# Five of 32 input products of the Mamba scans made by TensorE from six chunks on, weight and column loads in pieces, and two silus in separate slots

## The chip, the cores and the metric

The kernel runs on one core of a Trainium2 chip. The time is that of the whole launch in microseconds of the device, as the median of three runs. The engines are PE (TensorE), DVE (VectorE), ACT (ScalarE), POOL (GpSimd) and SP (SyncE, which here only issues transfers). Each takes its own instructions strictly in the order in which they are written.

## What is computed

Four layers of a network over x of 2 batches, 1024 tokens, 256 features. Layer 0 is a Mamba block, layer 1 a bidirectional one (a forward and a backward scan), layers 2 and 3 are attention. The scans of layers 0 and 1 are what the change touches:

```python
xt = jnp.transpose(x_in, (0, 2, 1))                       # layer 0 only: convolution over 4 tokens, then silu
u = jax.nn.silu(conv(xt) + conv_b)
x_dbl = jnp.einsum('bsd,ed->bse', u, x_proj_w)
dt_r, B, C = jnp.split(x_dbl, [DT_RANK, DT_RANK + N], axis=-1)      # N = 16 states
dt = jax.nn.softplus(jnp.einsum('bsr,dr->bsd', dt_r, dt_proj_w) + dt_proj_b)
def step(h, inp):
    dA = jnp.exp(dt_t[:, :, None] * A)
    h = h * dA + (dt_t * u_t)[:, :, None] * B_t[:, None, :]
    y = jnp.einsum('bdn,bn->bd', h, C_t)
    return (h, y)
y = (y + u * D_param) * jax.nn.silu(z)                    # z: the second half of the input projection
```

There are 512 channels and 16 states, so each token has 512 x 16 values of h.

## The kernel before, in words

**Chunks and steps.** The scans are cut into 12 chunks of 512 tokens (`WORK`, `NK` = 12): chunks 0 to 3 are layer 0 (two batches of two chunks), chunks 4 to 7 layer 1 of the first batch (forward 4 and 5, backward 6 and 7), chunks 8 to 11 the same of the second. A chunk has 32 steps (`HALVES`): two halves of the channels (256 channels each, as two blocks q = 0 and 1 of 128 partitions) times 16 states n. `at` counts all 384 steps, `h` those of a chunk. A chunk is "second" where it carries h on from the one before (1, 3, 5, ...). In the others ("first") ACT keeps the last value of each scan (`save`, L1976), and POOL waits for that.

**One step** goes through the engines like this:

1. PE `spread` (L1577): one matmul of 48 rows copies row n of B to all 128 partitions, into PSUM bank 2 or 3 in turn. It waits until DVE has read that bank two steps ago.
2. DVE `load` (L2161): w (= dt times u, in `ws`) times that bank, 128x1024, into a slot of `hbuf`, a ring of five (`RING`).
3. ACT `decays` (L1968): exp(dt * A) for q = 0 and q = 1, each 128x512, into PSUM bank 6 + q. It waits for the scan of the step before, which read that bank.
4. DVE `scan` (L2176): two scans of 128x512, q = 0 and q = 1, in place in the ring, with the bank of decays as factor.
5. POOL weighs the slot with row n of C (L1340), 128x1024, from `cbuf`, a ring of three that SP fills by `load_c` (L1094), 256 KB each. `load_c` of a step waits until POOL has weighed three steps ago.
6. PE `add_state` (L1598): four matmuls of 64x64 add the slot to the sums in banks 0 and 1.

**The order is written by hand.** In pass h of its loop, DVE runs load(at + 1) and scan(at), ACT the decays of at, POOL its product of at, PE spread(at + 2) and add_state(at - 2), SP load_c(at). After that each engine does the work "beside" the scan that falls due at slot h: generators `beside(j)` yield slot numbers, and what stands behind a yield is issued at that slot. These hold the projections of the next chunk (z at slots 4, 6, 8, 10 of a chunk ahead of a backward one, L1429; the projection to B, C and dt at 21 or 22, L1456; dt, L1463), the output projection of the last one (L1405), the layer norms of chunks 4, 5, 8 and 9 (in the chunk before each: POOL's L1219 and L1221 at slots 7 and 8, DVE's statistics of their result at slot 10, L2064), POOL's four products for dt and w at slot 27 (L1252, L1258), POOL's tap of the convolution in layer 0 (L1203, L1207, L1209), and the silus. For these ACT has to load another table and then the old one again (`silus`): z (L1729), then u (L1737) in layer 0. The decays of one step (`AHEAD`, slot 21 or 14) are made before that, into two spare banks.

**Loads beside chunk 0.** At slot 12 SP stores the conditioning, loads all weights of layer 1 (`in_w` to `wl1`, L1112, 3968 KB in one), two rows (L1076) and four small columns (`f_ada`, L1082, each of 512 single elements of 4 bytes). Its next `load_c` stands behind these. The columns of layers 2 and 3 are first read in chunk 2, the weights in chunk 3.

In the code block below, the lines are those of the profile.

## Time and profile before

| | us |
|---|---|
| median of three runs | 2138.95 (2136.35 to 2139.67) |
| the profiled execution | 2137.9 |
| its span, first to last instruction | 2136.1 |
| the scans, first load to last scan | 68.7 to 1477 |
| attention, after the scans | about 1479 to 2136 |
| mean granted clock of TensorE | 0.848 of full |

The chunks begin (first scan) at 72.4, 202.1, 320.6, 440.8, 565.6, 680.5, 791.9, 900.5, 1022.1, 1136.2, 1247.8 and 1357.0 us. A step takes 3.36 us in a first and 3.48 us in a second chunk where nothing is beside it. The profile gives the busy time of each engine, the waits with who ended them, and the instructions in order of time.

### The profile page before, as it was taken

Reading aid. Unit: us, or ns where it says so; the run is one execution under the profiler, and the core shown is the slowest. Engines: PE = TensorE matmul, PEld = TensorE weight load, DVE = VectorE, ACT = ScalarE, POOL = GpSimd, SP = SyncE. Lnnn points to the kernel's source line nnn. Section 1 sums busy time; section 2 is a strip of 40 time slices with the busy share of each in tenths; the row PEclk is TensorE's granted clock in tenths of the full one; section 3 lists DMA queues with packets and bytes.
Section 4 is the critical chain, followed back from the end, with each engine's and each line's share of the span. In section 5 each row is a group of like instructions: output and inputs, shape, how many; then the busy total and the mean of one; then the engine's idle time right before and its main releaser. Section 6 shows DMA issues by size and latency. Waiting matters only on the chain.

```text
span 2136.1 us, 22565 instructions
## 1 busy us (share of the span) xinstructions
PE 1728.3 (81%) x7664; PEld 588.8 (28%) x7664; DVE 1854.2 (87%) x2189; ACT 1199.4 (56%) x2147; POOL 1147.4 (54%) x584
## 2 busy tenths in 40 slices
PE   5776979789797777778787878787887899999986
PEld 2221313133231211122221112232663333333323
DVE  4688999899999999999999999999557888888803
ACT  3756565645656565555565655553462266666672
POOL 2667977877888887778888786864000000000000
PEclk9887979859687788878778778797998799999998
DMA  5142222122222222212222222321060522220001
...
DMA packets 80727, 143.41 MB, mean 67 GB/s; under 512 B 14587, under 2 KB 19643, under 8 KB 80076
## 3 DMA queue, kind: packets, MB, share of 16 engines
...
## 4 chain that ended last, share of the span: by engine, by line
DVE 46%; PE 33%; issue 10%; ACT 5%; POOL 4%; DMA 1%; SPq 1%; DVEq 0%; ACTq 0%; POOLq 0%
DVE hbuf L2176 27%; DVE hbuf L2161 11%; PE psum L688 6%; PE psum L654 5%; PE psum L674 4%; PE psum L1598 4%; PE psum L569 3%; POOL hbuf L1340 3%; DVE gain L969 2%; PE psum L558 2%; PE psum L1429 1%; PE psum L1405 1%; PE psum L1554 1%; PE psum L1577 1%; PE psum L1456 1%
## 5 line engine op out<-in xcount | busy, mean ns | idle before, releaser
L1340 POOL TENSOR_TENSOR hbuf<-hbuf,cbuf 128x1024 f32<-128x1024 f32 x384 | 902.1, 2356 | 286.6 <-DVE hbuf L2176 147.0
L1968 ACT ACTIVATE psum<-slots,cols 128x512 f32<-128x512 f32 x768 | 525.3, 687 | 450.6 <-DVE hbuf L2176 446.8
L1598 PE MATMUL psum<-hbuf,ident 64*64 64x512 f32 x3072 | 530.1, 768 | 211.6 <-POOL hbuf L1340 211.2
L2161 DVE TENSOR_TENSOR hbuf<-slots,psum 128x1024 f32<-128x1024 f32 x384 | 459.4, 1197 | 52.8 <-POOL slots L1258 30.3
L2176 DVE TENSOR_TENSOR_SCAN hbuf<-psum,hlast,hbuf 128x512 f32<-128x512 f32 x384 | 470.4, 1266 | 3.1 <-ACT psum L1968 3.0
L2176 DVE TENSOR_TENSOR_SCAN hbuf<-psum,hbuf 128x512 f32<-128x512 f32 x384 | 447.4, 1206 | 4.5 <-ACT psum L1968 4.4
L969 DVE TENSOR_REDUCE gain<-psum 128x1 f32<-128x512 f32 x512 | 315.7, 682 | 59.1 <-PE psum L654 58.7
L520 POOL COPY wl<-hbuf 128x512 f32<-128x512 f32 x8 | 4.8, 612 | 429.3 <-PE psum L688 400.7
L654 PE MATMUL psum<-slots 99*128 99x512 bf16 x512 | 197.1, 400 | 23.9 <-DVE gain L969 11.5
L1577 PE MATMUL psum<-bcs,pick 48*128 48x512 bf16 x384 | 171.0, 446 | 45.0 <-DVE hbuf L2161 42.8
L674 PE MATMUL psum<-slots 102*128 102x512 bf16 x512 | 194.4, 388 | 6.5 <-ACT xn_flat L852 1.7
L1598 PEld LDWEIGHTS psum<-hbuf,ident 64*64 64x64 f32 x3072 | 94.7, 154 | 366.7 <-POOL hbuf L1340 305.2
L852 ACT ACTIVATE slots<-psum 128x512 f32<-128x512 f32 x256 | 133.9, 626 | 62.4 <-PE psum L674 62.4
L1577 PEld LDWEIGHTS psum<-bcs,pick 48*128 48x128 bf16 x384 | 36.8, 96 | 378.8 <-DVE hbuf L2161 228.1
L852 ACT ACTIVATE xn_flat<-psum 128x512 f32<-128x512 f32 x128 | 70.3, 607 | 81.2 <-PE psum L674 81.2
L1429 PE MATMUL psum<-slots,wl 128*128 128x512 f32 x192 | 107.3, 693 | 0.0
L674 PEld LDWEIGHTS psum<-slots 102*128 102x128 bf16 x512 | 49.4, 98 | 141.6 <-issue 50.3
L654 PEld LDWEIGHTS psum<-slots 99*128 99x128 bf16 x512 | 51.3, 100 | 85.9 <-DVE gain L969 45.9
L1976 ACT ACTIVATE hlast<-hbuf 128x2 f32<-128x2 f32 x192 | 39.5, 206 | 63.0 <-DVE hbuf L2176 62.4
L688 PE MATMUL psum<-slots,wl 128*32 128x512 f32 x512 | 67.9, 651 | 7.4 <-issue 7.4
L1405 PE MATMUL psum<-w_gated,slots 128*128 128x256 f32 x256 | 68.4, 416 | 6.1 <-DVE slots L2184 6.1
L852 ACT ACTIVATE wl<-psum 128x512 f32<-128x512 f32 x128 | 71.0, 625 | 3.6 <-PE psum L674 3.5
...
## 6 DMA issues: line engine op xcount, KB each, us to landing
cbuf<-scr_c SPq DMA_DIRECT2D x384, 256.0 KB, 3.1
...
```

The source lines that it names most:

```text
L654: pe.matmul(psum[:, 4 + n % 4, :], st[0:K_MAX, 0, h, i * P:(i + 1) * P], st[0:K_MAX, 1, h, side * 512:side * 512 + 512], start=True, stop= ...
L674: pe.matmul(psum[:, 1 + n % 3, :], st[0:K_EXP, 1, h, i * P:(i + 1) * P], st[0:K_EXP, 0, h, a * 512:a * 512 + 512], start=True, stop=True). ...
L688: last = pe.matmul(psum[h * 32:h * 32 + 32, 0, :], v_quad[job % 2][:, ip * 2 + il, h, :], probs[g % 2][h][:, il * 512:il * 512 + 512], sta ...
L852: act.activation(probs[g % 2][h][:, il * 512:il * 512 + 512], psum[:, 1 + n % 3, :], ACT.Exp).then_inc(exped, 1)
L969: dve.tensor_reduce(half_max[:, n % 2, at:at + 1], psum[:, 4 + n % 4, :], AX.X, ALU.max).then_inc(maxed, 1)
L1340: pool.tensor_tensor(hs, hs, cbuf[:, at % CRING:at % CRING + 1, :].to_broadcast([P, 2, TC]), ALU.mult).then_inc(weighed, 1)
L1429: last = pe.matmul(ps, w[:, m, at:at + P], src[:, m, :], start=m == 0, stop=m == KD - 1)
L1577: pe.matmul(psum[:, 2 + at % 2, :], pick[:, n:n + 1].to_broadcast([3 * NS, P]), bcs[0:3 * NS, k % 2 * TC:(k % 2 + 1) * TC], start=True, st ...
L1598: last = pe.matmul(psum[side, bank, :], ident[rows_of, rows_of], hbuf[rows_of, at % RING, q, :], start=False, stop=n == NS - 1, skip_group ...
L1968: act.activation(decay_bank(at, q), dts[k % 2][:, e, :], ACT.Exp, scale=coefficient(WORK[k], e, n)).then_inc(decay, 1)
L2161: dve.tensor_tensor(hbuf[:, at % RING, :, :], ws[k % 2][:, 2 * p:2 * p + 2, :], psum[:, 2 + at % 2:3 + at % 2, :].to_broadcast([P, 2, TC]) ...
L2176: dve.tensor_tensor_scan(hs, decay_bank(at, q)[:, way], hs, hlast[:, e, n:n + 1] if c.second else 0.0, ALU.mult, ALU.add).then_inc(scanned, 1)
```

## The change

**Products by PE.** In chunks 5 to 10 (`PE_CHUNKS`) the steps h = 9, 11, 13, 27 and 29 (states 9, 11 and 13; `PE_SLOTS`) have no load and no spread. PE makes the product of w and B instead (`product`): for each q and each block of 128 tokens one matmul, f32, 128x128x128, with the transposed w (`wT`) as weights and a matrix that has B of the state on its diagonal (`diag_b`) as the moving side. q = 0 goes into bank 2 or 3, where the spread would have gone, q = 1 into bank 7. The scan reads this from PSUM and its decays from the ring slot in SBUF, where ACT now writes them. product(at, 0) is written in pass at - 1 behind add_state, product(at, 1) at the head of pass at, and it waits for the scan of step at - 1 to have read bank 7. The spread of the step after a run of such steps is written one pass later than before.

**What feeds it.** For each chunk PE turns four blocks of w (`turn_w`, four 128x128 transposes each, at slots 2, 3 and twice at 14 or 16), and ACT copies them out (`turned_w`, four of 128x512). SP writes three rows of B as the diagonals of three DRAM matrices (`store_diagonals`, 512 elements of 4 bytes each, slots 27, 29, 31 of the chunk before) and loads the three matrices, 256 KB each, at slot 3. The DRAM area is filled with zeros once (1.5 MB, slot 8 of chunk 1) from a small tile that POOL clears first. POOL's and ACT's split of B writes its remainder elsewhere, so that B stays; shapes and counts are as before.

**Loads.** The weights of layer 1 are loaded in eight pieces at slots 13 to 20 of chunk 0, and the four column loads stand in chunk 1, at slots 8, 9, 14 and 19 (the first yields 4, but stands behind the clearing at 8).

**Silus.** For chunks 1 to 3, ACT does the silu of u at slot 20 and that of z at slot 21; the table loads are the same two.

```diff
+PE_CHUNKS = range(5, NK - 1)
+PE_STATES = (9, 11, 13)
+PE_SLOTS = (9, 11, 13, 27, 29)
+def by_matmul(at):
+    k, h = divmod(at, HALVES)
+    return k in PE_CHUNKS and h in PE_SLOTS
...
         def decay_bank(at, q):
+            if by_matmul(at):
+                return hbuf[:, at % RING, q, :]
...
+        def product_bank(at, q):
+            return psum[:, 7 if q else 2 + at % 2, :]
...
+            def store_diagonals(k):
+                for i, n in enumerate(PE_STATES):
+                    yield 27 + 2 * i
...
+                    sp.dma_start(on_diagonal, values, allow_slow_non_contiguous=True).then_inc(diag_stored, 16)
...
+                if j in PE_CHUNKS:
+                    yield 3
+                    load_diagonals(j)
...
                 if j == 0:
                     yield 12
                     store_conditioning(1)
                     sp.wait_ge(grouped, done("ada", 1, 0))
-                    sp.dma_start(wl1[:, 0:NW1], w1).then_inc(ld_w1, 16)
                     load_conditioning_rows()
-                    load_film_columns()
+                    for n in range(W1_PIECES):
+                        yield 13 + n
+                        piece = slice(n * NW1 // W1_PIECES, (n + 1) * NW1 // W1_PIECES)
+                        sp.dma_start(wl1[:, piece], w1[:, piece]).then_inc(ld_w1, 16)
+                if j == 1:
+                    yield from load_film_columns()
...
+            def product(at, q):
+                k, h = divmod(at, HALVES)
+                p, n = divmod(h, NS)
+                i = PE_STATES.index(n)
+                pe.wait_ge(taken_act, taken(G["wT", k, 2 * p + q]))
+                pe.wait_ge(ld_diag[i], 16 * (k - PE_CHUNKS[0] + 1))
+                if q:
+                    pe.wait_ge(scanned, 2 * (at - 1) + 2)
+                else:
+                    before = max(m for m in range(at % 2, at, 2) if not by_matmul(m))
+                    pe.wait_ge(dbu, loaded(before))
+                    if by_matmul(at - 2):
+                        pe.wait_ge(scanned, 2 * (at - 2) + 1)
+                for j in range(TB):
+                    last = pe.matmul(product_bank(at, q)[:, j * P:(j + 1) * P], wT[:, j, q * P:(q + 1) * P], diag_b[i][:, j * P:(j + 1) * P],
+                                     start=True, stop=True)
+                last.then_inc(dbu_matmul, 1)
...
                     at = j * HALVES + h
-                    if at + 2 < TOTAL:
+                    if by_matmul(at - 1) and not by_matmul(at + 1):
+                        spread(at + 1)
+                    if by_matmul(at):
+                        product(at, 1)
+                    elif at + 2 < TOTAL and not by_matmul(at + 2):
                         spread(at + 2)
                     if at >= 2:
                         add_state(at - 2)
+                    if by_matmul(at + 1):
+                        product(at + 1, 0)
...
                         ahead(k)
-                        silus(k)
+                        act.preload_act_table_set("silu_and_others")
+                        silu_of_u(k)
+                        yield SILU0 + 1
+                        silu_of_z(k)
+                        act.preload_act_table_set("natural_log_exp_and_others")
...
-                    if at + 1 < TOTAL:
+                    if at + 1 < TOTAL and not by_matmul(at + 1):
                         load(at + 1)
```

PE in chunk 6, slots 7 to 10, before: L1577 is the spread, L1598 add_state (64x512 x4), L1429 the projection of z.

```order
L1577 MATMUL psum<-bcs,pick 128x512
L1598 MATMUL psum<-hbuf,ident 64x512 x4
L1577 MATMUL psum<-bcs,pick 128x512
L1598 MATMUL psum<-hbuf,ident 64x512 x4
L1429 MATMUL psum<-slots,wl 128x512 x2
L1577 MATMUL psum<-bcs,pick 128x512
L1598 MATMUL psum<-hbuf,ident 64x512 x4
```

The same place in the change: L1673 is the spread, L1721 add_state, L1510 z, L1699 the product.

```order
L1721 MATMUL psum<-hbuf,ident 64x512 x4
L1673 MATMUL psum<-bcs,pick 128x512
L1721 MATMUL psum<-hbuf,ident 64x512 x4
L1699 MATMUL psum<-wl 128x128 x4
L1510 MATMUL psum<-slots,wl 128x512 x2
L1699 MATMUL psum<-wl 128x128 x4
L1721 MATMUL psum<-hbuf,ident 64x512 x4
L1673 MATMUL psum<-bcs,pick 128x512
```

The spreads of steps 9 and 11 are gone; product(9, 0) has come between add_state and the projection of z, product(9, 1) behind it.

ACT in chunk 0, slots 20 to 22, before: L1968 x2 are the decays ahead, L1729 the silu of z, L1737 that of u, L1976 the save.

```order
L1968 ACTIVATE psum<-slots,cols 128x512 x2
L1742 ACT_TABLE_LOAD
L1729 ACTIVATE slots<-slots 128x2048
L1737 ACTIVATE slots<-slots 128x2048
L1747 ACT_TABLE_LOAD
L1976 ACTIVATE hlast<-hbuf 128x2
L1968 ACTIVATE psum<-slots,cols 128x512
```

In the change: L2119 are decays, L1873 the silu of u, L1865 that of z, L2127 the save.

```order
L2119 ACTIVATE psum<-slots,cols 128x512 x2
L1943 ACT_TABLE_LOAD
L1873 ACTIVATE slots<-slots 128x2048
L2127 ACTIVATE hlast<-hbuf 128x2
L1865 ACTIVATE slots<-slots 128x2048
L1947 ACT_TABLE_LOAD
L2119 ACTIVATE psum<-slots,cols 128x512
```

One save has come between the two silus, and u is first.

SP in chunk 0 at slot 12, before, and then the change (there L1113 is the store, L1119 the rows, L1138 load_c, L1189 a piece of the weights):

```order
L1070 DMA scr_ada<-slots 2x1792
L1112 DMA wl<-in_w 128x7936
L1076 DMA wl<-scr_ada 128x768 x2
L1082 DMA f_ada<-scr_ada 128x4x1 x4
L1094 DMA cbuf<-scr_c 128x512 x14
```

```order
L1113 DMA scr_ada<-slots 2x1792
L1119 DMA wl<-scr_ada 128x768 x2
L1138 DMA cbuf<-scr_c 128x512
L1189 DMA wl<-in_w 128x992
L1138 DMA cbuf<-scr_c 128x512
```

The weights now come in pieces between the load_c, and the column loads have left this chunk.

## Rows read from the trace of the kernel before

**Rows 1.** The page: busy us, share of the span and instructions of each engine

```profile
PE 1728.3 (81%) x7664; PEld 588.8 (28%) x7664; DVE 1854.2 (87%) x2189; ACT 1199.4 (56%) x2147; POOL 1147.4 (54%) x584
```

**Rows 2.** Waits of DVE: waited for, us in total, times, longest

```profile
DVE hbuf L2161 <- POOL slots L1258: 30.3, 1, 30.3
DVE hbuf L2161 <- PE psum L1577: 22.4, 9, 8.3
DVE hbuf L2176 <- ACT psum L1968: 7.4, 12, 2.4
```

**Rows 3.** Timeline, end of chunk 7: start, us, engine, line, [idle before <-releaser]

```profile
1007.07 1.20 DVE L2161 TENSOR_TENSOR hbuf<-slots,psum 128x1024 f32<-128x1024 f32 x1
...
1008.18 2.45 DVE L2176 TENSOR_TENSOR_SCAN hbuf<-psum,hlast,hbuf 128x512 f32<-128x512 f32 x2
...
1009.50 0.69 ACT L1968 ACTIVATE psum<-slots,cols 128x512 f32<-128x512 f32 x1 [1.06 <-DVE hbuf L2176]
...
1010.55 1.20 DVE L2161 TENSOR_TENSOR hbuf<-slots,psum 128x1024 f32<-128x1024 f32 x1
```

**Rows 4.** Busy time in chunks 5 to 10, all engines, then L2161 alone

```profile
680.00:1357.00 677.00, 523.39 (x2188) 134.10 (x2184) 675.80 (x625) 400.37 (x694) 550.11 (x265) 0.78 0.25 76
...
680.00:1357.00 677.00, 230.23 (x193) 0.78 0.25 76
```

**Rows 5.** Timeline, SP's queue at the start and in chunk 0, POOL, DVE

```profile
22.74 0.94 SPq L1145 DMA_DIRECT2D ada_cols<-scr_ada  x2
...
116.88 10.53 SPq L1082 DMA_DIRECT2D f_ada<-scr_ada  x4
...
132.83 2.34 POOL L1340 TENSOR_TENSOR hbuf<-hbuf,cbuf 128x1024 f32<-128x1024 f32 x1 [8.68 <-DMA cbuf<-scr_c]
...
141.29 1.22 DVE L2161 TENSOR_TENSOR hbuf<-slots,psum 128x1024 f32<-128x1024 f32 x1 [8.32 <-PE psum L1577]
```

**Rows 6.** Timeline, chunk 0 around the silus: ACT, POOL, PE, DVE

```profile
159.75 1.89 ACT L1737 ACTIVATE slots<-slots 128x2048 f32<-128x2048 f32 x1
...
163.31 6.96 POOL L1340 TENSOR_TENSOR hbuf<-hbuf,cbuf 128x1024 f32<-128x1024 f32 x3 [6.95 <-ACT hlast L1976]
...
167.61 5.65 PE L1456 MATMUL psum<-slots 128*96 128x512 f32 x8
...
163.84 2.34 DVE L2176 TENSOR_TENSOR_SCAN hbuf<-psum,hbuf 128x512 f32<-128x512 f32 x2 [2.39 <-ACT psum L1968]
...
173.62 1.22 DVE L2161 TENSOR_TENSOR hbuf<-slots,psum 128x1024 f32<-128x1024 f32 x1 [4.08 <-PE psum L1577]
```

**Rows 7.** Timeline, chunk 2 around the silus: POOL and DVE

```profile
398.87 1.26 POOL L1209 TENSOR_TENSOR slots<-slots 128x512 f32<-128x512 f32 x1
...
405.06 1.22 DVE L2161 TENSOR_TENSOR hbuf<-slots,psum 128x1024 f32<-128x1024 f32 x1 [5.19 <-PE psum L1577]
```

**Rows 8.** Timeline of PE: transposes, then chunk 6 around slot 8

```profile
961.75 1.94 PE L1419 MATMUL psum<-ident,xn_flat 128*128 128x128 f32 x8
...
1503.89 1.91 PE L551 MATMUL psum<-ident,wl 128*128 128x128 f32 x16
...
817.51 1.98 PE L1598 MATMUL psum<-hbuf,ident 64*64 64x512 f32 x8 [1.59 <-POOL hbuf L1340]
819.43 3.78 PE L1429 MATMUL psum<-slots,wl 128*128 128x512 f32 x4
823.14 0.59 PE L1577 MATMUL psum<-bcs,pick 48*128 48x512 bf16 x1
823.65 1.09 PE L1598 MATMUL psum<-hbuf,ident 64*64 64x512 f32 x8
```

**Rows 9.** Timeline of POOL and DVE at slots 8 to 10, chunks 7 and 8

```profile
942.52 2.35 POOL L1221 TENSOR_TENSOR xn_flat<-xn_flat,shift 128x1024 f32<-128x1024 f32 x1
...
944.98 1.38 DVE L2064 BATCH_NORM_STATS2 stats<-xn_flat 128x6 f32<-128x256 f32 x4
...
1062.67 1.41 DVE L2064 BATCH_NORM_STATS2 stats<-xn_flat 128x6 f32<-128x256 f32 x4 [0.53 <-POOL xn_flat L1221]
```

122 lines of the change are left out of this document (104 added, 18 removed).

## The prediction, as it was put on record

> **What bounds the kernel now.** I read the busy shares first [rows 1]: DVE leads with 87%, PE follows with 81%. A share over the whole span hides the stages, so next come the windows over chunks 5 to 10 [rows 4]: of 677 us DVE is busy 675.8, PE 523, POOL 550, ACT 400. There DVE is the bound and nobody makes it wait. The waits of DVE [rows 2] say the same from the other side: in the whole scan stage loads waited for PE only 9 times, 22.4 us in total, 8.3 of it in one place, and scans for ACT 7.4 us. So a gain can come from DVE instructions taken away in chunks 5 to 10, and from those few waits in chunks 0 to 3. The attention behind the scans is not touched; it moves as a whole.
>
> **The price of a load.** In a quiet step [rows 3] a load starts at 1007.07, the pair of scans at 1008.18, the next load at 1010.55. The instructions overlap a little, so a load costs 1.11 us of DVE's time, not its 1.20, and a pair of scans 2.37. The change removes 5 loads in each of 6 chunks: 30 x 1.11 = 33.3 us. The scan still reads one operand from PSUM and one from SBUF (they change places), so I leave its price; whether the place of the operands matters no row shows, and I allow 0.1 us for each of 60 scans either way, 6 us, in the range. If all 30 loads came off the path and nothing else moved, that is the ceiling of this part.
>
> **Who must now be on time.** Without a load in front, scan(at, 0) follows scan(at - 1, 1) at once, and two engines lose slack.
>
> ACT: it starts its decays 0.06 us after the scan that frees the bank and takes 0.69 (the pair of scans starts at 1008.18, its first is over at about 1009.44, ACT starts at 1009.50) [rows 3]. With as much for the way back it needs about 0.85 us, the scan in between lasts 1.18. That fits, by 0.3 us (0.2 with a save ahead of it). I take nothing for it. The copies of the turned w (four of about 0.7 a chunk) and the split of B with its new address stand beside scans in ACT's and POOL's idle time; nothing.
>
> PE: four products or transposes of 128x128 f32 take 0.96 us at the full clock (16 records, two for each matmul, in 1.91) and 1.94 at half of it (8 in 1.94) [rows 8]; add_state 1.09 and 1.98, a spread 0.59 at half clock (0.4 I take at full). A step of this kind adds 8 matmuls and drops one spread, and a chunk adds 16 transposes: 5 x 1.9 + 3.9 - 5 x 0.4 = 11.4 us at full clock, to 87 of 113 us (523/6) [rows 4]. So PE has the room on average, and the question is order. Product(at, 1) may start when scan(at - 1, 1) is over and is wanted after one load and one scan, 1.11 + 1.18 = 2.3 us later; alone it fits at either clock. Where a z projection stands between product(at, 0) and it (slots 8 and 10 of chunks 5, 6, 9, 10), it does not always. In chunk 6 [rows 8] add_state starts at 817.51 and z runs 3.78 us from 819.43, at the half clock up to about 823.6. With product(9, 0) ahead of z, z ends at about 824.4 and product(9, 1) at 825.4; DVE, with load(9) gone, wants it at about 822.2. That is 3.2 us lost against 5.55 won in this chunk. The same walk gives 1.3 in chunk 5, 1.5 in chunk 10 and 0.5 in chunk 9, where PE keeps the full clock. Sum 6.5. At slots 27 and 29 PE now gets work where it ran at half clock before; at full clock everything fits, in the first microseconds at half clock up to 1 us may go. I take 2 us for six chunks.
>
> **A gain that cannot be had.** In chunks 7 and 8 DVE's statistics at slot 10 wait for POOL's L1221. In chunk 7 it ends at 944.87 and DVE starts at 944.98 with no idle time, just in time; in chunk 8 DVE already waits 0.53 us [rows 9]. POOL is busy without a gap ahead of this, so it doesn't come earlier. Two loads (9 and 11) go ahead of that place, so 2 x 1.11 in each of two chunks is turned into waiting: 4.4 us.
>
> Chunks 5 to 10: 33.3 - 6.5 - 2.0 - 4.4 = 20.4 us.
>
> **Loads of chunk 0.** The four column loads hold SP's queue for 10.53 us [rows 5], while two column loads of the same form, with no weights ahead of them, took 0.94. So it is the queue full of 3968 KB of weights that holds them, and load_c stands behind. POOL waits 8.68 for its row of C, and DVE, by way of PE, 8.32 for POOL: one chain. With pieces of 496 KB between the load_c, each an eighth of that, 1.3 us, and the columns elsewhere, all of the 8.32 goes. What is late next is POOL with its convolution, as in chunk 1, where DVE's only waits of over 0.3 us are one for ACT; all its waits for PE are nine [rows 2]. In chunk 1 the clearing of 1.5 MB and four column loads of 0.5 us come in. The clearing takes some 4 to 6 us of the queues, my estimate from the 10.53 us for which 3968 KB held them; POOL is behind its convolution there and asks for rows late. Nothing, at worst 2 us.
>
> **Silus.** In chunk 0 POOL waits 6.95 us for the save behind both silus; add_state, and behind it the projection L1456 (5.65 us at half clock), come late, and DVE waits 4.08 for its spread [rows 6]. With the save between the silus it comes where the second silu started, at 159.75, and POOL starts at about 160.1 and not 163.31: 3.2 us earlier, and so does PE. I take 3.5 us with the clock that the shorter gap saves, between 2.5 and 4.4. The 2.39 us for the decays stay: ACT has the same work up to them. In chunk 2 the wait of 5.19 us isn't the silus': POOL does its whole convolution in one go there up to 400.1, and PE waits for POOL [rows 7]; that remains, and u now waits for the convolution with z behind it, by my walk without a loss. Chunk 1 is a second chunk without saves: nothing.
>
> **Sum.** 20.4 + 8.3 + 3.5 = 32.2 us off the profiled execution of 2137.9 gives 2105.7. The median of the runs lies 1.05 above that execution, so I predict **2106 us** (own range 2099 to 2114).
>
> **Rivals.**
>
> *All of it is had (2096).* If PE stays at the full clock in these chunks, the 6.5 and 2.0 shrink to about 0: 2106 - 8.5 = 2097, and with the last microsecond of the silus 2096. For it: the products fill PE's gaps. Against: at slot 8 of chunk 6 PE waited for POOL 1.59 us and ran at half clock though its share there was high [rows 8], and POOL's pace does not change. The Trainium skill, "TensorE: Matmul & The Clock Gate", Part 1, says that the throttled clock is the default and that activity releases it; by that rule more work makes each matmul cheaper, and the sum would be this one. In the rows PE goes back to the full clock at 823.6 after it has worked without a gap from 817.5, which agrees.
>
> *PE's order eats the products (2126).* One late product delays the scan, and add_state behind it keeps PE late for the next. If each of the 30 products costs as much as it saves, the 20.4 go: 2106 + 20 = 2126. For it: 3.2 us in a single place of chunk 6, and half clock at slots 26 to 31, where a product, two add_states and a spread (3.88 + 3.96 + 0.59) would take PE 8.4 us against the 5.85 of two DVE passes (2.37 + 3.48). Against: busy without a gap, PE should leave the half clock.
>
> *Slower (2155).* The transfers for the diagonals hold SP's queue, with load_c behind them. Place: three stores of 512 single elements at slots 27 to 31 and 768 KB of loads at slot 3, in each of six chunks. Price: in chunk 0 a hold of 10.53 us cost DVE 8.32 [rows 5], so 2.2 us are covered; six holds as long as that one cost 6 x 8.3 = 50, and 2106 + 50 = 2156, less the change of the places where POOL is behind anyway: 2155. It turns the change into a loss from 2.2 + 33/6 = 7.7 us of hold a chunk. Against: the columns of the same form took 0.47 us each to issue. These read from DRAM, though, and ours write to it; no row shows that. The Trainium skill, "DMA: Bandwidth & Descriptors", Specifications, says that below 512 B a transfer becomes a read-modify-write, which speaks for this rival; no row here shows such a store.
>
> *The edit in chunk 0 doesn't do what it says (2117).* If the wait there comes back elsewhere (the clearing in chunk 1, the pieces ahead of load_c), 8.3 + 3.5 go: 2118 with the products as forecast, 2117 with what the clock gives.
>
> **Chances.** Forecast 0.43, all of it 0.19, PE's order 0.20, chunk 0 0.07, slower 0.08; 0.03 for something that I don't see. The range is to hold 8 in 10: from 2094, which takes in the upper case and part of the 6 us of the scans, to 2128, which takes in PE's order; the slower case and the tails stay out. A measurement of this kernel tells apart about 0.2%, 4.3 us. Faster than that: all but the slower case, the unknown and a little of PE's order, 0.87; the same 0.04; slower 0.09.
>
> **What would show it.** In the profile of the change: 354 loads instead of 384, and chunks 5 to 10 together 656 to 657 us long instead of 676.5. Right: no DVE wait near 8 us in chunk 0, a wait of about 2.2 us of L2064 for POOL in chunk 7 and 2.7 in chunk 8, waits of scans for the products of 1 to 3 us at slot 9 of chunks 5, 6 and 10, none at 27 and 29. Wrong: POOL waiting for cbuf in chunks 5 to 11 (the slower rival), scans waiting for products at all five slots (PE's order), scans longer than 1.27 us, or scans waiting for ACT in each step without a load.

## The result and the profile after

| | before | after |
|---|---|---|
| median of the runs, us | 2138.99 (6 runs, 2136.35 to 2142.39) | 2122.32 (6 runs, 2116.56 to 2127.02) |
| profiled execution, us (span) | 2137.9 (2136.1) | 2122.75 (2121.0) |
| first scan starts, us | 72.4 | 73.2 |
| chunk 0, us | 129.7 | 115.3 |
| chunk 1, us | 118.5 | 124.2 |
| chunks 2 to 4, us | 359.9 | 359.7 |
| chunks 5 to 10, us | 676.5 | 668.8 |

The ratio is 0.992, with a 95% interval of 0.9907 to 0.9933: faster, by 16.7 us where I had forecast 33 (2138.95 to 2106). Chunk lengths run from the first scan of a chunk to the first scan of the next. Chunk 0 gave 14.4 us (forecast 11.8), chunks 5 to 10 gave 7.8 (forecast 20.4), and chunk 1 lost 5.7 (forecast nothing).

Where the products are, the window over chunks 5 to 10 answers to [rows 4]. Columns: the stretch, its length, then busy time and number of records of PE, PE's weight loads, DVE, ACT and POOL, the granted clock, DMA share and GB/s. Second, the waits of DVE in it (us in total, times, longest):

```profile
672.38:1341.17 668.79, 542.16 (x2734) 198.13 (x2730) 644.52 (x596) 410.24 (x717) 549.26 (x265) 0.90 0.29 84
```

```profile
DVE hbuf L2331 <- ACT psum L2119: 7.7, 8, 3.4
DVE hbuf L2331 <- PE psum L1699: 6.4, 6, 2.5
DVE stats L2215 <- POOL xn_flat L1301: 4.9, 2, 2.8
DVE hbuf L2312 <- PE psum L1673: 3.1, 4, 1.2
DVE hbuf L2312 <- issue: 1.7, 2, 1.0
```

(L2312 is the load, L2331 the scan, L1699 the product, L1673 the spread, L1721 add_state, L2119 a decay, L2132 the copy of the forward sums, L1421 POOL's weighing, L1301 its L1221 of before.) DVE's busy time fell from 675.8 to 644.5: the loads are gone. But DVE, which had waited 1 us in all, now waits 23.8. The gain was made and then three quarters of it turned into waiting, nearly half of that for decays and spreads (7.7 and 3.1 us), for which I had allowed 2 us at most.

In chunk 1 the clearing of the diagonals' buffer shows. First the DMA issues of 210 to 240 us (KB each, median us from issue to landing), then the chain on POOL, PE and DVE (start, us, engine, line, what, idle before and for whom):

```profile
scr_diag<-wl SPq DMA_DIRECT2D x1, 1539.0 KB, 19.3
cbuf<-scr_c SPq DMA_DIRECT2D x6, 256.0 KB, 6.6
f_ada<-scr_ada SPq DMA_DIRECT2D x2, 2.0 KB, 15.8
```

```profile
233.97 2.35 POOL L1421 TENSOR_TENSOR hbuf<-hbuf,cbuf 128x1024 f32<-128x1024 f32 x1 [7.20 <-DMA cbuf<-scr_c]
...
236.36 1.98 PE L1721 MATMUL psum<-hbuf,ident 64*64 64x512 f32 x8 [7.77 <-POOL hbuf L1421]
...
242.41 1.22 DVE L2312 TENSOR_TENSOR hbuf<-slots,psum 128x1024 f32<-128x1024 f32 x1 [5.28 <-PE psum L1673]
```

The clearing is 19.3 us on its way, and a load of 256 KB beside it takes 6.6 us to land, where in a quiet stretch (500 to 540 us, eleven loads) it takes 3.2. The hold on the queue that I feared for the small stores came from this one.

The other loss is at the start of chunk 9. PE, ACT and DVE there (its first scan is at 1120.84):

```profile
1111.38 0.60 PE L1673 MATMUL psum<-bcs,pick 48*128 48x512 bf16 x2
1117.13 1.99 PE L1721 MATMUL psum<-hbuf,ident 64*64 64x512 f32 x8 [5.16 <-POOL hbuf L1421]
...
1123.96 2.07 PE L1544 MATMUL psum<-wl,wdts 64*128 64x512 f32 x2
1125.82 0.63 PE L1673 MATMUL psum<-bcs,pick 48*128 48x512 bf16 x1
1126.38 1.98 PE L1721 MATMUL psum<-hbuf,ident 64*64 64x512 f32 x8
...
1128.43 1.02 ACT L2132 ACTIVATE slots<-psum 128x1024 f32<-128x1024 f32 x1 [4.42 <-PE psum L1721]
...
1131.30 1.28 DVE L2331 TENSOR_TENSOR_SCAN hbuf<-psum,hlast,hbuf 128x512 f32<-128x512 f32 x1 [3.43 <-ACT psum L2119]
```

Read it backwards. DVE waits for the decays of slot 2. They stand in ACT's queue behind the copy of the last chunk's sums, and that waits 4.42 us for PE's last add_state. PE is late because POOL had let it stand idle for 5.16 us and because, from 1117.13 on, it works at half clock (1.99 us for an add_state that takes 1.09 at the full one). The windows of the same stretch show the clock (length, PE busy, clock, DMA):

```profile
1113.20:1117.10 3.90, 0.00 (x0) 0.83 0.06 22
...
1117.13:1136.50 19.37, 19.37 (x65) 0.51 0.43 122
```

POOL, at last, is late because of what stands at its slot 27: two pairs of operations (1109.84 to 1114.74) and then five weighings in a row. At the end of the weighing of slot 28 its lag behind the scans was 6.2 to 6.9 us before and is 7.4 to 8.6 now. A part of this is DMA: in chunks 6, 7, 8 and 10 POOL waits 0.9 to 1.5 us for its row of C just ahead of these operations (before only once, 0.95 us in chunk 10). In chunks 5 and 9, where it doesn't wait, the lag still grew by 1.2 us. It catches up by a step's length less 2.35 us; a step without a load is 2.3 to 2.4 us long. So a load saved behind slot 27 takes POOL's time to catch up away.

### The profile page after: what moved, and what is told of

Its sections match the earlier page's. It is cut to its first block, busy times and chain, and to the rows that moved or that the text cites. A ratio compares the mean times of both kernels' runs of the same rounds, so it can differ in the third digit from the quotient of the medians.

```text
span 2121.0 us, 23810 instructions
## 1 busy us (share of the span) xinstructions
PE 1739.7 (82%) x8210; PEld 651.4 (31%) x8210; DVE 1822.9 (86%) x2159; ACT 1211.9 (57%) x2171; POOL 1147.5 (54%) x585
## 4 chain that ended last, share of the span: by engine, by line
PE 40%; DVE 34%; issue 9%; POOL 8%; ACT 7%; DMA 2%; SPq 0%; DVEq 0%; ACTq 0%; POOLq 0%
DVE hbuf L2331 19%; DVE hbuf L2312 7%; PE psum L1721 6%; PE psum L731 6%; POOL hbuf L1421 6%; PE psum L697 5%; PE psum L717 4%; PE psum L612 3%; PE psum L1510 3%; DVE gain L1012 2%; PE psum L601 2%; PE psum L1673 1%; PE psum L1518 1%; PE psum L1537 1%; DMA cbuf<-scr_c 1%
## 5 line engine op out<-in xcount | busy, mean ns | idle before, releaser
L1421 POOL TENSOR_TENSOR hbuf<-hbuf,cbuf 128x1024 f32<-128x1024 f32 x384 | 901.8, 2358 | 272.9 <-DVE hbuf L2331 141.2
L2119 ACT ACTIVATE psum<-slots,cols 128x512 f32<-128x512 f32 x708 | 485.5, 689 | 392.0 <-DVE hbuf L2331 387.9
L1721 PE MATMUL psum<-hbuf,ident 64*64 64x512 f32 x3072 | 491.6, 715 | 172.8 <-POOL hbuf L1421 172.2
L2312 DVE TENSOR_TENSOR hbuf<-slots,psum 128x1024 f32<-128x1024 f32 x354 | 422.1, 1193 | 49.8 <-POOL slots L1338 30.3
L2331 DVE TENSOR_TENSOR_SCAN hbuf<-psum,hlast,hbuf 128x512 f32<-128x512 f32 x354 | 432.5, 1263 | 8.7 <-ACT psum L2119 8.7
L2331 DVE TENSOR_TENSOR_SCAN hbuf<-psum,hbuf 128x512 f32<-128x512 f32 x354 | 411.1, 1200 | 8.8 <-ACT psum L2119 8.8
L697 PE MATMUL psum<-slots 99*128 99x512 bf16 x512 | 197.1, 400 | 23.9 <-DVE gain L1012 11.5
L1721 PEld LDWEIGHTS psum<-hbuf,ident 64*64 64x64 f32 x3072 | 91.0, 147 | 318.3 <-POOL hbuf L1421 255.4
L1673 PE MATMUL psum<-bcs,pick 48*128 48x512 bf16 x354 | 147.5, 423 | 34.2 <-DVE hbuf L2312 32.4
L1673 PEld LDWEIGHTS psum<-bcs,pick 48*128 48x128 bf16 x354 | 32.9, 95 | 291.3 <-issue 150.5
L1510 PE MATMUL psum<-slots,wl 128*128 128x512 f32 x192 | 104.8, 680 | 6.9 <-ACT wl L1833 6.9
L1699 PE MATMUL psum<-wl 128*128 128x128 f32 x480 | 70.8, 294 | 14.0 <-DVE hbuf L2331 10.4
L2127 ACT ACTIVATE hlast<-hbuf 128x2 f32<-128x2 f32 x192 | 39.7, 207 | 68.7 <-DVE hbuf L2331 68.4
L1699 PEld LDWEIGHTS psum<-wl 128*128 128x128 f32 x480 | 61.9, 201 | 46.9 <-issue 40.7
```

Source lines behind the costliest of these rows:

```text
L697: pe.matmul(psum[:, 4 + n % 4, :], st[0:K_MAX, 0, h, i * P:(i + 1) * P], st[0:K_MAX, 1, h, side * 512:side * 512 + 512], start=True, stop= ...
L1421: pool.tensor_tensor(hs, hs, cbuf[:, at % CRING:at % CRING + 1, :].to_broadcast([P, 2, TC]), ALU.mult).then_inc(weighed, 1)
L1510: last = pe.matmul(ps, w[:, m, at:at + P], src[:, m, :], start=m == 0, stop=m == KD - 1)
L1673: pe.matmul(psum[:, 2 + at % 2, :], pick[:, n:n + 1].to_broadcast([3 * NS, P]), bcs[0:3 * NS, k % 2 * TC:(k % 2 + 1) * TC], start=True, st ...
L1699: last = pe.matmul(product_bank(at, q)[:, j * P:(j + 1) * P], wT[:, j, q * P:(q + 1) * P], diag_b[i][:, j * P:(j + 1) * P], start=True, st ...
L1721: last = pe.matmul(psum[side, bank, :], ident[rows_of, rows_of], hbuf[rows_of, at % RING, q, :], start=False, stop=n == NS - 1, skip_group ...
```

## Experiments

All times are medians, with the ratio to the kernel before and its 95% interval. "5 to 10" is the length of these chunks in the profiled execution, 676.5 before. I lean on it more than on the medians, since the first scan starts at 72 us in some traces and at 77 in others (last section). But it is the length in one execution.

| kernel | us | ratio | 5 to 10 | loads gone there |
|---|---|---|---|---|
| the change | 2122.3 | 0.992 (0.9907 to 0.9933) | 668.8 | 30 |
| e1, clearing in pieces | 2119.1 | 0.9906 (0.989 to 0.9922) | 668.6 | 30 |
| e2, no products | 2126.1 | 0.9946 (0.9932 to 0.9959) | 676.5 | 0 |
| e3, slots 9, 11, 13 | 2128.2 | 0.9948 (0.9933 to 0.9963) | 672.2 | 18 |
| e4, slots 27, 29 | 2131.1 | 0.9958 (0.9943 to 0.9973) | 679.6 | 12 |
| e5, e1 + sums later | 2118.6 | 0.9908 (0.9895 to 0.9922) | 664.6 | 30 |
| e6, e1 + PE kept busy | 2119.6 | 0.9913 (0.99 to 0.9927) | 669.2 | 30 |
| e7, e1 at 8, 10, 12 | 2128.5 | 0.9952 (0.9939 to 0.9964) | 675.6 | 18 |
| e8, loads of chunk 0 alone | 2132.4 | 0.9966 (0.9952 to 0.998) | 676.5 | 0 |
| e9, e5 + product first | 2112.8 | 0.9881 (0.9865 to 0.9896) | 658.7 | 30 |
| e10, e9 at 11, 13, 19, 21 | 2148.2 | 1.0041 (1.0028 to 1.0053) | 698.6 | 24 |
| e11, e9 + slot 25 | 2107.0 | 0.9856 (0.9842 to 0.9869) | 658.9 | 36 |
| e12, e9 + slot 7 | 2121.2 | 0.9921 (0.9908 to 0.9935) | 669.1 | 36 |

**e1: the clearing.**

```diff
-                if j == 1:
-                    yield 8
...
-                    sp.dma_start(everything, src).then_inc(diag_cleared, 16)
+                if j in (2, 3, 4):
+                    for b in range(2):
+                        yield (11, 21)[b]
+                        sp.wait_ge(no_b_ready, 1)
+                        piece = scr_diag[b, j - 2, :].rearrange("(p g c) -> p g c", p=P, c=(TC + 1) // 3)
...
+                        sp.dma_start(piece, src).then_inc(diag_cleared, 16)
```

> The change, with the clearing of the diagonals' buffer in DRAM cut into six pieces of 257 KB, two in each of chunks 2, 3 and 4 (slots 11 and 21), in place of one store of 1539 KB in chunk 1. Theory A (the one long store, 19.3 us until it landed, kept the loads of C's rows and with them POOL, PE and DVE): the DVE wait of 5.28 us in chunk 1 goes, chunk 1 is 118.5 to 119 us long, and the kernel takes 2117.0 us. Each piece takes about 3.2 us, and POOL asks for its row two scans ahead, so the pieces cost nothing. Rival B (the wait in chunk 1 comes from the four column loads, or from POOL's convolution, which is late there anyway): the wait stays where it is and the time stays at 2122. Rival C (the pieces hold the queue as the one did, a sixth each): the 5.3 us come back in six places, 2121 to 2123.

Chunk 1 took 118.5 us, as before the change. The wait was the clearing's; theory A. Chunks 2 to 4, where the pieces are, took 361.8, 2.2 us more than in the change. This is not the pieces' doing: the kernel without products and without any clearing has 361.9 (e2), and e11 and e12, with pieces, have 359.6 and 359.8. The kernel gained 3.3 us in the medians, 5.7 in the chunk. A piece of 256.5 KB lands in 4.6 us, not in 3.2.

**e2: the change without products.** The range of product chunks is empty, the clearing left out.

```diff
-PE_CHUNKS = range(5, NK - 1)
+PE_CHUNKS = range(0)
```

> The change without its products: no chunk multiplies on PE, so there is no clearing, no storing and loading of diagonals and no turned w either; all 384 products are DVE's again. What is left is chunk 0 (weights in pieces, columns in chunk 1, the two silus apart) and the split of B. If the chunk lengths add up as I read them (chunk 0 shorter by 14.4, the start later by 0.9, chunks 5 to 10 as before), it takes 2139.0 - 13.5 = 2125.4 us: then the products with their clearing are worth 3 us net, 7.8 in chunks 5 to 10 less 5.3 in chunk 1. By my forecast of chunk 0 (11.8 us) it is 2127.2. The rival, that a part of the gain in chunk 0 is only possible since the products give slack later, would put it above 2130.

2126.1 against the 2125.4 of the sum. Chunks 5 to 10 are back at 676.5, and DVE waits 1 us in them, as before. So the products are worth 7.8 us there, as the chunk lengths said, and about 4 us net of their clearing.

**e3 and e4: one half of the slots each.**

```diff
-PE_SLOTS = (9, 11, 13, 27, 29)
+PE_SLOTS = (9, 11, 13)
```

and in e4

```diff
-PE_SLOTS = (9, 11, 13, 27, 29)
+PE_SLOTS = (27, 29)
```

> The change with products only at slots 9, 11 and 13: the loads at slots 27 and 29 are DVE's again, 12 loads of 1.11 us, 13.3 us in all. Theory P (from slot 27 on POOL is the bound: its lag behind the scans is 7.3 to 8.6 us at slot 28 and still 3.9 to 5.5 at the end of the chunk, against 6.2 to 6.6 and 2.7 to 3.4 before, and DVE gets the saved time back as waits at slots 0 to 2 of the next chunk): about 7 us come back as waits that go (3.1 for the spreads, 4.5 of the 7.7 for ACT), so it takes 2122.3 + 13.3 - 7.5 = 2128 us, and these waits are gone. Rival Q (the waits at the chunks' starts come from the products at 9 to 13 or from the turning of w): they stay, and it takes 2135.6. Rival R (the products at 27 and 29 pay nothing): 2122.

> The change with products only at slots 27 and 29: the loads at slots 9, 11 and 13 are DVE's again, 18 loads, 20.0 us. Of these 6.0 us are lost now as waits for late products at slots 9 and 11 and 4.9 as waits of the statistics for POOL in chunks 7 and 8 (0.5 before), so the net value of the three slots is 20.0 - 6.0 - 4.4 = 9.6 us, and it takes 2122.3 + 9.6 = 2132 us. If the two halves of the products don't disturb each other, its gain over the kernel without products and that of the three-slot kernel add up to the gain of all five. Rival: the time won at slots 9 to 13 is what runs up against ACT and POOL at the chunk's end (DVE comes early), then this loses less, 2126 to 2128, and the waits at the chunks' starts go though 27 and 29 are still multiplied.

In the profiled executions the three slots take 4.3 us off chunks 5 to 10, and the two slots **add** 3.1 us, although they take 12 loads off DVE. The two windows, e3 and e4:

```profile
671.10:1343.31 672.21, 544.41 (x2551) 178.59 (x2551) 656.84 (x608) 410.25 (x717) 549.86 (x265) 0.83 0.27 84
```

```profile
675.61:1355.17 679.56, 542.74 (x2464) 167.81 (x2460) 663.76 (x613) 410.00 (x717) 549.27 (x265) 0.84 0.28 82
```

and the waits of DVE in e4:

```profile
DVE hbuf L2331 <- ACT psum L2119: 8.3, 4, 3.4
DVE hbuf L2312 <- issue: 2.5, 2, 1.7
DVE hbuf L2312 <- PE psum L1673: 1.9, 3, 0.9
DVE hbuf L2331 <- PE psum L1699: 1.8, 1, 1.8
```

DVE is busy 663.8 us where it was 675.2 without products: 11.5 us of work is gone, but it waits 15.2 us where it waited 1. More than half of that are three waits for ACT at slot 2 of chunks 6, 9 and 10. In e3, without the two slots, the waits for ACT are 2.5 us. So the value of the two slots depends on what happens at the chunk's start. Theory P holds in its mechanism, and e3 met its time (2128), though one wait of 2.16 us for ACT stayed, at slot 2 of chunk 6. e4 met the first expectation (2132). What failed is the claim that the gains of the halves add up: -4.3 and +3.1 against -7.8 together. On top of the other three, the two slots gave 3.4 us (672.2 to 668.8) for 12 loads of 13.3 us.

The loss of 3.1 us is that of one execution, and an unlucky one: it was the slowest of e4's eleven (2120.5 to 2136.7 us), 5.6 us above their median, and e3's lay 3.4 below its own. The medians of e3 and e4 are 2.1 and 5.0 us above that of e2, and of this the clearing in chunk 1 explains 3.8 and 3.5. That leaves a gain of 1.7 for the three slots and a loss of 1.5 for the two, both within what the runs can tell apart. So it is shown that the two slots alone gain nothing; that they lose is not.

The size of the wait for ACT goes with PE's clock. These are the waits of over 0.5 us at slot 2 of chunks 6, 9 and 10 in the change, e1, e3, e4 and e6. PE was busy for 10.00 of the 10 us ahead of each of these scans:

| kernel, chunk | clock in the 10 us ahead of the scan | wait for ACT, us |
|---|---|---|
| change and e1, 6 and 10 | 0.78 to 0.79 | 0.89 to 0.92 |
| e6, 6 and 9 | 0.78, 0.79 | 1.00, 0.53 |
| e4, 6 | 0.77 | 1.19 |
| e3, 6 | 0.50 | 2.16 |
| e6, 10 | 0.50 | 2.92 |
| e4, 10 | 0.50 | 3.31 |
| change, e1 and e4, 9 | 0.50 | 3.42 to 3.43 |

No run changes the clock alone, so that it sets the size is argued from this table, not shown.

**e5: the order in ACT's queue.** The copy of the forward sums one slot later:

```diff
-                    if h == 1 and j and j - 1 not in GATED:
+                    if h == 2 and j and j - 1 not in GATED:
                         keep_sums(j - 1, 1)
```

> The cleared-in-pieces kernel (2119.1 us), with ACT's copy of the forward sums (keep_sums) one slot later in ACT's queue: behind the decays of slot 2 and no longer ahead of them. In chunks 6, 9 and 10 this copy stands waiting for PE's last add_state (in the second-half kernel 4.10 us at 1251.45) with the decays of slot 2 behind it, and DVE waits for them (0.9, 3.4 and 0.9 us with all five slots). Theory O (the order in ACT's queue makes DVE wait): these 5.2 us go, PE waits a little for the sums' bank instead, and it takes 2114 us. Theory K (PE at half clock behind its gap is late by itself, and DVE waits for the next thing PE makes, the spreads): the waits only change their name, from ACT to PE's spreads, and it takes 2118 to 2120.

No wait of over 0.5 us for ACT is left at the chunks' starts; chunk 9 takes 107.7 instead of 111.9, and chunks 5 to 10 take 664.6, 4.1 less. Theory O by the trace; a part came back as waits for products (8.1 us against 6.1 in e1). The median moved by 0.4 us only and lies where theory K had it (2118 to 2120), so the runs by themselves could not show it; its profiled execution was the fastest of its four (2115.0, with the first scan at 75.9). What a later run adds: in e12, which has this order too, the clock was 0.50 for the 10 us ahead of slot 2 of chunk 9, and the wait for ACT there was 0.20 us and not 3.4. Another 1.8 us of waits followed at slots 3 and 4, 1.5 of them for spreads, so theory K has a part in it.

**e6: filling PE's gap.** The spread of slot 30 nine times:

```diff
+                for _ in range(9 if k in PE_CHUNKS and h == 30 else 1):
+                    last = pe.matmul(psum[:, 2 + at % 2, :], pick[:, n:n + 1].to_broadcast([3 * NS, P]),
+                                     bcs[0:3 * NS, k % 2 * TC:(k % 2 + 1) * TC], start=True, stop=True)
+                last.then_inc(bcast, 1)
```

> The cleared-in-pieces kernel, with the spread of slot 30 done nine times over in PE's queue at slot 28 of chunks 5 to 10: the same matmul into the same bank, 8 x 0.39 = 3.1 us more of work for PE in the gap of 4 to 5.6 us in which it now waits for POOL (POOL works off what stands at slot 27). Nothing else is changed. Theory K (the gap lets the clock fall to half, and in chunk 9 it stays there for 19 us although PE works without a gap from 1117 on, so that PE is late at the chunk's start): with the gap filled the granted clock stays at 1.0 there, the ACT waits of 3.4 and 0.9 us and the spread waits of 2.1 us at the chunks' ends shrink, and it takes 2113 to 2115 us, though PE has more to do. Rival P (POOL alone is late; the clock doesn't matter): the waits stay and it takes 2119, or 2120 to 2122 where the filling is in the way.

Nothing gained; the time is rival P's (2119 to 2122). At the start of chunk 9 the stretch at half clock was shorter (7 us instead of 20), and the wait of 3.4 us shrank to 0.53; but chunk 10 had it instead (2.92), and the waits for products rose from 6.1 to 8.2. I had put the work in front of the gap, not in it: POOL's burst came after, and PE still waited 3.7 us for it (1105 to 1120 us) and fell to half clock behind that:

```profile
1112.00:1115.00 3.00, 3.00 (x25) 1.00 0.26 87
1115.00:1118.00 3.00, 0.49 (x2) 1.00 0.00 0
1118.00:1121.00 3.00, 1.84 (x8) 0.53 0.20 46
```

So this run doesn't show what a held clock would give; only that here too the long wait stands where the clock was low.

**e7: slots 8, 10, 12**, where no projection stands between the halves of a product:

```diff
-PE_STATES = (9, 11, 13)
-PE_SLOTS = (9, 11, 13, 27, 29)
+PE_STATES = (8, 10, 12)
+PE_SLOTS = (8, 10, 12)
```

> The cleared-in-pieces kernel, with three products a chunk at slots 8, 10 and 12 (states 8, 10 and 12) in place of five at 9, 11, 13, 27 and 29. At these slots the z projection no longer stands between the two halves of a product. Eighteen loads of 1.11 us go, 20.0 us; the odd slots (three-slot kernel) gave only 4.3 of it, with 5.1 us lost to late products, 4.4 to the statistics behind POOL, 2.5 to ACT at the chunks' starts and 2.7 at slot 3 of chunks 7 and 8. Theory Z (late products are a matter of the place beside z): the 5.1 us go, the rest stays, chunks 5 to 10 take 676.5 - 9.4 = 667 us, and the kernel 2117. Rival (PE is late at these slots for add_state and POOL, wherever z stands): the same as the odd slots, 2124 with the cleared pieces.

Worse than the odd slots: 675.6 against 672.2, so 18 loads gave 0.9 us, with 8.5 us of waits for products (9 times). Theory Z (2117) fell, or at least was not the main thing, and the time is 4.5 us above the rival's 2124 too. No second half waits for z any more, but now the first half of the product of slot 12 is late, by 0.95 to 1.57 us in all six chunks. It stands in PE's queue behind the add_state of slot 9, and there POOL's lag is 6.2 us in chunk 5 and 4.7 in chunk 6, since two steps without a load lie behind it. That is the theory that e9 tests.

**e8: the loads of chunk 0 alone**, in the kernel before:

```diff
-                    sp.dma_start(wl1[:, 0:NW1], w1).then_inc(ld_w1, 16)
                     load_conditioning_rows()
-                    load_film_columns()
+                    for n in range(W1_PIECES):
+                        yield 13 + n
+                        piece = slice(n * NW1 // W1_PIECES, (n + 1) * NW1 // W1_PIECES)
+                        sp.dma_start(wl1[:, piece], w1[:, piece]).then_inc(ld_w1, 16)
+                if j == 1:
+                    yield from load_film_columns()
```

> The kernel before with one part of the change: the weights of layer 1 in eight pieces and the column loads in chunk 1. No silus apart, no products, no clearing. My sum gave 8.3 us to this and 3.5 us to the silus; chunk 0 gave 14.4 in the changed kernel (129.7 to 115.3 us). Theory: the wait of 8.32 us of DVE goes and the wait of 4.08 behind the silus stays, so chunk 0 takes 121 us and the kernel 2139.0 - 8.7 = 2130.3. Rival (the loads' wait hid a part of what the silus cost, so that most of the 14.4 is the loads' alone): chunk 0 at 116 to 118, 2126. Rival (the gain comes with the silus): above 2134.

Chunk 0 takes 119.7 us, nearer to the theory's 121 than to the rival's 116 to 118: 10.0 of the 14.4 are the loads', 4.4 the silus'. The split is good to about 1 us: by the clock of the span chunk 0 ends 10.2 us earlier in e8 and 13.5 in the change, which leaves 3.3 for the silus, and in the other kernels with both edits chunk 0 takes 115.2 to 116.8 us. The wait behind the silus is still there as before, 4.03 us; in the change it is gone:

```profile
163.44 1.22 DVE L2167 TENSOR_TENSOR hbuf<-slots,psum 128x1024 f32<-128x1024 f32 x1 [4.03 <-PE psum L1583]
```

The profiled execution (2127.7) is 10.2 us below that of before; the median, 2132.4, is less so because four of its six executions lie 4.8 us higher.

**e9: the product first.** e5, and in PE's queue:

```diff
+                    if by_matmul(at + 1):
+                        product(at + 1, 0)
                     if at >= 2:
                         add_state(at - 2)
-                    if by_matmul(at + 1):
-                        product(at + 1, 0)
```

> The cleared-in-pieces kernel with the forward sums copied one slot later (as in e5), and in PE's queue each first half of a product ahead of the add_state of the same step, not behind it; the same five slots. Theory L (products come late because they stand in PE's queue behind an add_state, which waits for POOL's weighed tile, and POOL lags 4 to 7 us behind the scans at just these slots, 9 to 11 and 28 to 31): the waits of scans for products, 6 to 7 us in chunks 5 to 10, go but for the second halves that stand behind z (about 2 us), and chunks 5 to 10 take 664.6 - 4.5 = 660 us, against 668.6 with neither edit. The waits of the statistics for POOL in chunks 7 and 8 (4.9 us) and of slot 3 (1.7) stay. Time 2114. Rival Z (it is the projection z in front of the second halves): the waits stay at 6, 664.6 us, time 2118. Rival (what is won is waited for at POOL's next tile, since POOL takes 2.33 us a step and DVE without a load 2.37): some of it comes back as waits for spreads at the chunks' ends, 662 to 664.

658.7 us for chunks 5 to 10 (expected 660), and 2112.8 us (expected 2114). Slots 10 and 11 of chunk 6, which begins at 779.30 us in the changed kernel and at 778.66 in e9; PE's rows in the changed kernel, with DVE's at slot 11, and then in e9:

```profile
813.02 1.09 PE L1721 MATMUL psum<-hbuf,ident 64*64 64x512 f32 x8 [0.98 <-POOL hbuf L1421]
814.04 1.16 PE L1699 MATMUL psum<-wl 128*128 128x128 f32 x8
815.04 1.88 PE L1510 MATMUL psum<-slots,wl 128*128 128x512 f32 x4
816.76 1.05 PE L1699 MATMUL psum<-wl 128*128 128x128 f32 x8
...
817.92 1.22 DVE L2331 TENSOR_TENSOR_SCAN hbuf<-hbuf,psum 128x512 f32<-128x512 f32 x1 [1.39 <-PE psum L1699]
```

```profile
809.47 1.16 PE L1699 MATMUL psum<-wl 128*128 128x128 f32 x8
811.41 1.09 PE L1721 MATMUL psum<-hbuf,ident 64*64 64x512 f32 x8 [0.78 <-POOL hbuf L1421]
812.43 1.98 PE L1510 MATMUL psum<-slots,wl 128*128 128x512 f32 x4
814.25 1.05 PE L1699 MATMUL psum<-wl 128*128 128x128 f32 x8
...
815.41 1.22 DVE L2331 TENSOR_TENSOR_SCAN hbuf<-hbuf,psum 128x512 f32<-128x512 f32 x1 [0.85 <-PE psum L1699]
```

In the first, add_state waits for POOL, and the first half, z and the second half stand behind it, 3.8 us of work after its own 1.0. In the second the first half is done while POOL is still at work, and the second half comes 1.9 us earlier by the chunk's clock; what is left of the wait, 0.85 us, is z behind the add_state. The waits for products, e5 and then e9:

```profile
DVE hbuf L2331 <- PE psum L1699: 8.1, 10, 1.5
```

```profile
DVE hbuf L2331 <- PE psum L1699: 3.2, 3, 1.5
```

Those of chunk 9 are gone. This is the cause of the late products at slots 9 and 11: POOL's lag handed on by PE's queue, with z on top, at full clock. One wait has another cause: at slot 27 of chunk 8 it was 1.53 us in e5 and is 1.46 in e9, and there PE runs at half clock (2.07 us for the first half of a product).

**e10: slots 11, 13, 19 and 21**, where POOL has caught up. There are four diagonals, so the clearing has eight pieces (at slots 5, 12 and 19) and the stores stand at slots 27 to 30:

```diff
-PE_STATES = (9, 11, 13)
-PE_SLOTS = (9, 11, 13, 27, 29)
+PE_STATES = (3, 5, 11, 13)
+PE_SLOTS = (11, 13, 19, 21)
```

> As e9, with four products a chunk at slots 11, 13, 19 and 21 (states 3, 5, 11 and 13), none at 9, 27 and 29. These are slots at which POOL has caught up with the scans (its lag is 2.5 to 2.8 us there in chunk 5, 2.7 to 4.1 in the others) and behind the statistics of slot 10. Theory P (a load saved pays only where POOL has slack: behind slot 27 and ahead of the statistics it is given back): 24 loads x 1.11 = 26.6 us, of which 1 to 3 us are lost at slot 21 behind two u projections and at 11 behind z, so chunks 5 to 10 take 676.5 - 24.5 = 652 us and the kernel 2107. The rival by the count of loads alone (each load pays the same, with the products ahead of add_state): 24 in place of 30 loads gives less than e9, chunks 5 to 10 at 664 us and 2118. The rival by which POOL's work is the bound of the whole chunk, wherever a load is saved: 664 too, with waits for POOL at slots 24 to 31.

A plain miss: 698.6 where I expected 652, and both rivals missed as well (664). At 11 and 13 the steps are short (2.2 to 2.4 us) and no product is late in chunks 5, 6, 9 and 10. At 19 and 21 the second half of the product stands behind the u projections. Chunk 6, slot 21, PE and DVE:

```profile
851.64 3.70 PE L1510 MATMUL psum<-slots,wl 128*128 128x512 f32 x8
855.18 1.05 PE L1699 MATMUL psum<-wl 128*128 128x128 f32 x8
856.16 1.09 PE L1721 MATMUL psum<-hbuf,ident 64*64 64x512 f32 x8
857.18 1.96 PE L1537 MATMUL psum<-slots,wl 128*96 128x512 f32 x4
859.07 0.60 PE L1673 MATMUL psum<-bcs,pick 48*128 48x512 bf16 x2
...
856.34 1.22 DVE L2331 TENSOR_TENSOR_SCAN hbuf<-hbuf,psum 128x512 f32<-128x512 f32 x1 [4.00 <-PE psum L1699]
859.50 1.22 DVE L2312 TENSOR_TENSOR hbuf<-slots,psum 128x1024 f32<-128x1024 f32 x1 [1.93 <-PE psum L1673]
```

Two projections in one go take 3.70 us at the full clock; DVE waits 4.00 for the product and 1.93 more for the next spread, which stands behind the low-rank projection. In all six chunks scans wait 28.7 us for products and loads 11.6 us for spreads, where I had allowed 1 to 3 us. So POOL's slack is not enough: PE has to be free of long work between the halves too.

**e11: e9 with slot 25 as well.**

```diff
-PE_SLOTS = (9, 11, 13, 27, 29)
+PE_SLOTS = (9, 11, 13, 25, 27, 29)
```

> As e9 (2112.8 us, chunks 5 to 10 in 658.7), with a sixth product a chunk at slot 25, by state 9's diagonal, which is there anyway: six more loads off DVE, 6.7 us. Slot 25 lies ahead of POOL's work of slot 27, where POOL has two small operations beside each weighed tile (lag 2.5 to 4 us). Theory P (ahead of slot 27 POOL can still follow, so a load pays there; what is lost is its lag at slots 28 to 31): most of it is had, chunks 5 to 10 take 653 to 655 us, the kernel 2108. Rival (POOL and PE are at their limit from slot 24 to the end of the chunk: the dt projections at half clock, the parts of B, two products): the products at 25 and 27 come late, as at slots 19 and 21 in e10, and it takes 2113 or more.

The fastest of all by its median, 2107.0, and still the sixth product gives nothing: chunks 5 to 10 take 658.9, as in e9. DVE is busy 6.3 us less (638.2 against 644.4), and its waits for ACT are 7.2 us instead of 1.7:

```profile
DVE hbuf L2331 <- ACT psum L2119: 7.2, 8, 1.5
```

They lie at slots 24 and 26. No product is late at 25 or 27, so the rival's reason didn't come true either. With load 25 gone scan 24 follows scan 23 at once, its decays are wanted 1.1 us earlier, and ACT has other work of the step ahead of them in its queue (at slot 24 of chunks 5 and 9, where the waits are 1.46 us each, the skip diagonals, 1.26 us). Another 2.0 us are a longer wait at slot 4 of chunk 8 (2.97 us, 0.96 in e9), where PE makes the output projection at half clock; e1, without slot 25, has 2.34 there, so I don't count it to the sixth product. The profiled executions differ by 5.6 us; the start of the scans (72.3 against 76.6) is 4.3 of it and no work of this change. I can't claim the median for slot 25.

**e12: e9 with slot 7 as well**, and with the four diagonals' clearing and stores placed as in e10:

```diff
-PE_STATES = (9, 11, 13)
-PE_SLOTS = (9, 11, 13, 27, 29)
+PE_STATES = (7, 9, 11, 13)
+PE_SLOTS = (7, 9, 11, 13, 27, 29)
```

> As e9, with a sixth product a chunk at slot 7 (states 7, 9, 11 and 13, a fourth diagonal to store and load: 256 KB more a chunk at slot 3, and one store more). In chunks 7 and 8 it lies ahead of the statistics that wait for POOL and gives nothing; in the other four 4 x 1.11 = 4.4 us. Theory L (with the product ahead of add_state only the projection z in front of a second half is left, which costs 0.85 us in two of the chunks): 654 to 656 us for chunks 5 to 10, 2109 to 2110 in all. Rival (four products in a row of six steps leave POOL behind, which takes 2.33 us a step and has its own operations at slots 8 and 9): waits for PE or POOL at slots 9 to 13 take it back, 2112 to 2114. Rival (the fourth load of 256 KB lands too late or holds the loads of C): POOL waits for cbuf and it is above 2114.

10.4 us more than e9 in chunks 5 to 10, and 2121.2 us in all; none of the three had that. Scans wait 13.9 us for products (11 times). In chunks 5 and 6 (106.6 and 105.0 us) the saved load and the waits at slots 9 and 11 cancel to a tenth, which is the second rival in kind. But the loss lies in chunks 7, 8 and 9: 2.3 and 2.6 us at slot 7 of chunks 7 and 8, where an output projection (1.99 us) stands between the halves of the product, as the u projections do in e10, and 3.4 us at slot 27 of chunk 8, with PE at half clock (2.07 and 1.91 us for the halves).

## Why the prediction was right, and where it was not

The direction was right, and the median lies in the range that was to hold 8 in 10 (2094 to 2128), though not in the forecast's own (2099 to 2114); the gain was half of the forecast. The sum has a slip of its own: 2105.7 and 1.05 make 2106.75, not 2106. Its steps:

- **The price of a load**, 33.3 us for 30. DVE's busy time fell by 31.3. 2 us too much; the scans didn't get longer (those that read a product take 1204 and 1264 ns, without and with a value carried in, the others of the same kernel 1199 and 1262), so the allowance for the operands' places was not needed.
- **Late products**, 6.5 us. Measured 6.4, six times, but this was luck. I had them at slot 9 of chunks 5, 6 and 10, with 3.2 at half clock in chunk 6 and 0.5 in chunk 9; it was slot 11 of those, 1.39 at full clock in chunk 6, and 2.51 at slot 9 of chunk 9. The step went through PE's queue without asking when add_state, in front of the product, gets its tile from POOL. e9 shows that this is what makes them late at these slots.
- **Slots 27 and 29**, 2.0 us. This is the step that failed. With them scans waited 7.7 us for ACT (2.5 without them, e3), 5.2 of it at slot 2 of chunks 6, 9 and 10, and loads 3.1 for spreads (none in e3). Of their 13.3 us of loads 3.4 were had on top of the other slots, so 9.9 were lost and not 2.0; alone they gained nothing (e4). Two sentences were wrong. "ACT ... needs about 0.85 us ... I take nothing for it" is right for a step in which ACT has nothing else in its queue, and I didn't look at the chunk's start, where the copy of the sums waits for PE. And "busy without a gap, PE should leave the half clock" did not hold in time at chunk 9: 19.37 us without a gap at 0.51.
- **The statistics**, 4.4 us: 4.9 after, 0.5 before. Right, by place and size (2.12 and 2.82 against 2.2 and 2.7).
- **Chunk 0**, 8.3 + 3.5: measured 10.0 + 4.4 (e8), good to about 1 us. Right, 2.6 us too small.
- **Chunk 1**, nothing, at worst 2 us: measured 5.7. The term was mis-sized. I had estimated the clearing at 4 to 6 us from a load of 3968 KB that held the queue for 10.53. It took 19.3 for 1539 KB. A store of 2304 rows of 684 bytes to DRAM is not a weights load, and no row of before had one; I should have bounded it from above, not by its bytes.

For chunks 5 to 10 the sum is 12.6 us off: 10.0 of waits more than forecast (23.8 against 12.9 and the 0.9 of before), 2.0 by the price of the loads, 0.6 in waits that the rows don't name.

Of the rivals, *PE's order eats the products* was nearest: 2126 against 2122.3. It had the effect right (what is saved is waited for) and the reason partly: not each product costs what it saves, but those at 27 and 29 nearly do (3.4 us left of 13.3). *All of it is had* failed. The Trainium skill, "TensorE: Matmul & The Clock Gate", Part 1, by which activity releases the throttled clock, is half borne out. The mean clock of these chunks rose from 0.78 to 0.90, and PE was busy only 19 us more, where the added work was 68 us by the prediction's prices at full clock (6 x 11.4, an estimate). But at the chunks' ends DVE's lead made PE's gaps longer in four of six (4.5 to 4.7 us before, 5.2 to 5.6 there), and behind the gap the clock was low while PE worked without a pause. *Slower by DMA* didn't come in its size: a diagonal's store takes 0.65 us to issue and a chunk's three loads land in 4.7 us each. But its sign, POOL waiting for cbuf, did show: four times and 4.7 us in all, just ahead of what stands at slot 27, where POOL has the least slack. No run moves these stores alone, so what they cost stays open. In size it came in chunk 1, by the clearing. *The edit in chunk 0 doesn't do what it says* (2117) had named that place: 5.7 us came back there, while chunk 0 kept its 14.4.
